# A mixture-of-experts tail on one core: the experts' rows are added by accumulating scatters to x that was stored before, in place of a gather, a weighting pass and a store behind the last expert

## The reference, cut to what matters

```python
h = _layernorm(x) * (1 + cb) + sb              # cb, sb, gb: one row of 128 values per batch
logits = h @ Wg                                 # 8 experts
vals, idx = top_k(softmax(logits), 2)
w = vals / (sum(vals) + 1e-9)                   # two weights per token
# each (token, choice) pair takes the next of 256 places of its expert, or none if it is full
for e in range(8):
    ye = gelu(h @ W1[e] + b1[e]) @ W2[e] + b2[e]    # 128 -> 512 -> 128
    out = out + combine[:, e][:, None] * ye
x = x + gb * out
```

## Time and profile before

| | before |
|---|---|
| median of 3 runs | 833.43 us (833.16 to 837.02) |
| profiled execution, its own time | 835.61 us |
| its span in the trace | 833.9 us |
| busy in the span | PE 718.4, DVE 643.0, POOL 586.7, ACT 491.7 us |
| mean granted TensorE clock | 0.923 |

### The profile page before, as it was taken

One profiled execution on the slowest core, in us unless ns is written; L12 is line 12 of the kernel. 1 busy time (PEld: TensorE's weight loads), 2 busy tenths in 40 slices (PEclk: granted clock), 3 DMA queues, 4 the chain that ended last, 5 costly groups with the idle time before them and its releaser, 6 DMA issues.

```text
span 833.9 us, 34140 instructions
## 1 busy us (share of the span) xinstructions
PE 718.4 (86%) x14802; PEld 655.3 (79%) x14803; DVE 643.0 (77%) x1057; ACT 491.7 (59%) x786; POOL 586.7 (70%) x429
## 2 busy tenths in 40 slices
PE   5577768736799999999999999999999999886997
PEld 2257567725689998988988888889988989785897
DVE  4894645527889999999988999899999999857215
ACT  4766315514675685767577666667766766637520
POOL 4243067866398989898988888888788989831750
PEclk9676659986999999999999999999999999975999
DMA  7832243411052000000000000000000000062128
GB/s 180 234 81 59 55 105 96 88 54 40 5 143 70 7 7 10 7 7 7 6 6 7 23 4 3 4 16 4 4 17 3 4 4 17 17 207 69 49 71 277
DMA packets 61598, 43.01 MB, mean 52 GB/s; under 512 B 22272, under 2 KB 54288, under 8 KB 61456
## 3 DMA queue, kind: packets, MB, share of 16 engines
q1 hardware_dynamic: 58128, 34.07, 14.7%
q0 software_dynamic: 3328, 6.82, 3.4%
HBM read 26.72 MB, written 14.16 MB: 49 GB/s over the span
## 4 chain that ended last, share of the span: by engine, by line
PE 71%; DVE 9%; issue 7%; POOL 5%; ACT 4%; DMA 2%; SPq 1%; POOLq 1%; DVEq 0%; ACTq 0%
PE psum L1875 19%; PE psum L1975 7%; PE psum L1930 7%; PE psum L1908 7%; PE psum L1966 4%; PE psum L1923 4%; PE psum L1937 4%; PE psum L1945 3%; POOL arena L561 2%; PE psum L1673 2%; PE psum L1916 2%; PE psum L2202 2%; PE psum L2226 2%; PE psum L2191 1%; PE psum L1733 1%
## 5 line engine op out<-in xcount | busy, mean ns | idle before, releaser
L1875 PE MATMUL psum<-hT,w_qkv 128*128 128x128 f32 x1408 | 173.4, 280 | 1.7 <-DVE arena L1424 1.2
L1875 PEld LDWEIGHTS psum<-hT,w_qkv 128*128 128x128 f32 x1408 | 164.0, 194 | 4.9 <-DVE arena L1424 1.4
L609 POOL TENSOR_TENSOR arena<-arena,small 128x1024 f32<-128x1024 f32 x56 | 106.0, 1914 | 50.5 <-DVE small L1437 50.5
L588 POOL TENSOR_TENSOR arena<-arena 128x1024 f32<-128x1024 f32 x56 | 106.7, 1906 | 12.4 <-ACT arena L952 12.1
L574 POOL TENSOR_TENSOR arena<-arena 128x1024 f32<-128x1024 f32 x56 | 106.6, 1903 | 0.0
L1430 DVE TENSOR_REDUCE small<-arena 128x16 f32<-128x1024 f32 x60 | 73.1, 1218 | 9.5 <-ACT arena L941 7.3
L613 POOL TENSOR_TENSOR arena<-arena 128x1024 f32<-128x1024 f32 x28 | 65.9, 2353 | 14.6 <-DVE arena L1457 14.5
L1418 DVE TENSOR_REDUCE small<-psum 128x16 f32<-128x1024 f32 x60 | 72.8, 1214 | 3.4 <-PE psum L1975 3.3
L921 ACT ACTIVATE arena<-psum 128x1024 f32<-128x1024 f32 x28 | 28.7, 1026 | 72.6 <-PE psum L1875 72.6
L561 POOL DMA_INDIRECT arena<-h_rows,route x40 | 40.3, 1008 | 43.9 <-DVE route L1275 32.0
L1424 DVE TENSOR_TENSOR arena<-psum,small 128x1024 f32<-128x1024 f32 x60 | 70.4, 1214 | 0.1
(11 more groups left out here) (325 smaller groups left out, 1651.2 us busy)
## 6 DMA issues: line engine op xcount, KB each, us to landing
y_rows<-hT SPq DMA_DIRECT2D x8, 512.0 KB, 6.4
arena<-y_rows SPq DMA_DIRECT2D x8, 512.0 KB, 7.1
o_rows<-arena SPq DMA_DIRECT2D x9, 256.0 KB, 2.4
x_sb<-in_L_attn_u SPq DMA_DIRECT2D x8, 256.0 KB, 4.4
arena<-in_W_inT SPq DMA_DIRECT2D x16, 128.0 KB
arena<-in_W_out SPq DMA_DIRECT2D x64, 32.0 KB
h_rows<-arena SPq DMA_DIRECT2D x4, 512.0 KB, 3.2
h_rows<-hT SPq DMA_DIRECT2D x8, 256.0 KB, 2.3
```

Source lines behind the costliest of these rows:

```text
L588: pool.tensor_tensor(x3, x3, lr[:, tile_of(t) * 32 + k * H:tile_of(t) * 32 + k * H + H].unsqueeze(2).to_broadcast([P, H, D]), ALU.mult).th ...
L609: pool.tensor_tensor(z4, z4, r3.unsqueeze(3).to_broadcast([P, 8, 2, CH]), ALU.mult).then_inc(done, 1)
L1875: mm = pe.matmul(ps[bank][:, p * P:(p + 1) * P], w_qkv[:, j * HD + p * P:j * HD + (p + 1) * P], hT[:, at:at + P], start=True, stop=True)
```

## The change

- **Output.** `out` has 128 rows more at its front, which take what belongs to no token and are cut off on the host as a slice. SP stores x in it during the attention, chunk by chunk beside h (`store_x`), and 128 rows of x into the front; the zero fill of `y_dram`, the read back, the final pass, `x_final` and the last stores are gone. `store_rows` issues two DMAs per chunk in place of one, since rows now lie in token order.
- **Scatter.** `scatter_rows` adds to `out` in DRAM (`compute_op=ALU.add`). As a token has two experts, POOL now waits before each expert's pair for the pair before it to have landed. `AHEAD` is 5.
- **Weights by place.** What is scattered must be weighted and gated. POOL splits the weights into three bf16 parts and multiplies them into the one-hot choice (`weights_by_slot`), ahead of its wait for the ids and of the gathers. PE runs a second pass of 64 products over `pos_hot` (`weights_of_slots`) behind the ids pass and behind POOL; four dummy products follow in place of 18. DVE puts each place's weight under its batch (`batch_of_slot`), PE turns that (`turn_weights`). SP copies the gates to 16 rows per batch with 8 DMAs, ACT makes 16 tables of them (`gate_tables`), and `slots_second` has one more product of 256 columns per expert, which gives weight times gate. DVE has one more multiplication per expert.
- **Layer 0.** The bf16 one-hot is computed directly, before the f32 one; `columns(1)` goes behind the ids pass.

The diff's core:

```diff
-AHEAD = 6
+AHEAD = 5
...
-            sp.wait_ge(x_added, 1)
-            for n in range(2 * BP):
-                r0 = P + n * NC * P
-                sp.dma_start(y_dram[r0:r0 + NC * P, :].rearrange("(t p) c -> p t c", p=P),
-                             hT[:, T * P:(T + 1) * P].unsqueeze(1).to_broadcast([P, NC, C])).then_inc(y_zeroed, 16)
...
             def store_rows(c):
                 sp.wait_ge(h_ready, c + 1)
-                sp.dma_start(h_dram[1].rearrange("(b t p) c -> p b t c", b=BP, p=P)[:, :, c, :], second_rows(c)[0]).then_inc(h_stored[0], 16)
+                for h in range(2):
+                    sp.dma_start(by_chunk(h_dram[1], h, c), second_rows(c)[0][h * CH:(h + 1) * CH]).then_inc(h_stored[0], 16)
+
+            def store_x(c):
+                for h in range(2):
+                    sp.dma_start(by_chunk(A["out"][P:, :], h, c), group_tiles(c)[1][h * CH:(h + 1) * CH]).then_inc(x_stored, 16)
 
             for c in range(NC - 1):
                 store_rows(c)
+                store_x(c)
+            sp.dma_start(A["out"][0:P, :], x_sb[:, 0:C]).then_inc(x_stored, 16)
...
+            store_x(NC - 1)
+            sp.wait_ge(wk_set, BP + 1)
+            for b in range(B):
+                at = b % 2 * CH
+                sp.dma_start(gate_rows[b:P:B, :], mod_of(1, b // 2, GB)[at:at + 2 * E]).then_inc(gates_in, 16)
+            sp.wait_ge(x_stored, 32 * NC + 16)
             for u in range(2):
                 sp.wait_ge(y_scattered[u], 16 * E)
-            for n in range(2 * BP):
-                sp.dma_start(back1[:, n // 2 * 2 * W8:(n // 2 + 1) * 2 * W8].rearrange("p (k h x) -> p k h x", k=2, h=2)[:, :, n % 2, :],
-                             y_dram[P:, :].rearrange("(p k n t) c -> p k n (t c)", k=2, n=2 * BP, t=NC // 2)[:, :, n, :]
-                             ).then_inc(y_half[n][0], 16)
...
-            pool.wait_ge(h_stored[0], 32 + 16 * NC)
+            te = lambda ap: ap.rearrange("p (t e) -> p t e", e=E)
+            over_e = lambda ap: ap.unsqueeze(2).to_broadcast([P, ap.shape[1], E])
+
+            def weights_by_slot():
+                parts = weight_parts.rearrange("p (m t) -> p m t", m=3)
+                chain.link(pool.tensor_copy(parts[:, 0], wk[:, :]))
+                chain.link(pool.tensor_tensor(weight_rest, wk[:, :], parts[:, 0], ALU.subtract))
+                chain.link(pool.tensor_copy(parts[:, 1], weight_rest))
+                chain.link(pool.tensor_tensor(weight_rest, weight_rest, parts[:, 1], ALU.subtract))
+                chain.link(pool.tensor_copy(parts[:, 2], weight_rest))
+                chain.link(pool.tensor_tensor(part_w.rearrange("p (m j t) -> p m j t", m=3, j=2),
+                                             parts.unsqueeze(2).to_broadcast([P, 3, 2, 2 * T]),
+                                             of_tile.rearrange("p (j t) -> p j t", j=2).unsqueeze(1).to_broadcast([P, 3, 2, 2 * T]), ALU.mult))
+                for n in range(6):
+                    last = pool.tensor_tensor(te(weight_rhs[:, n * 2 * T * E:(n + 1) * 2 * T * E]), te(oh1),
+                                             over_e(part_w[:, n * 2 * T:(n + 1) * 2 * T]), ALU.mult)
+                last.then_inc(rhs_ready, 1)
+
+            pool.wait_ge(wk_set, BP + 1)
+            pool.wait_ge(rhs_ready, 5)
+            weights_by_slot()
+            pool.wait_ge(h_stored[0], 32 + 32 * NC)
             pool.wait_ge(ids_set, BP + 1)
             def fetch_rows(e):
 
@@ -697,14 +721,16 @@
             def scatter_rows(e):
 
                 pool.wait_ge(o_ready, TILES0 + 1 + e + 1)
+                if e > 0:
+                    pool.wait_ge(y_scattered[(e - 1) % 2], 32 * ((e - 1) // 2 + 1))
                 apart(pool)
                 for t in range(2):
-                    pool.indirect_dma_start(y_dram[:, :], rows_of(ids_i, e + (2 * E + E * t)), o1_st[e][:, t * C:(t + 1) * C], None,
-                                            bounds_check=P + 2 * B * L - 1, oob_is_err=False).then_inc(y_scattered[e % 2], 16)
+                    pool.indirect_dma_start(A["out"][:, :], rows_of(ids_i, e + (2 * E + E * t)), o1_st[e][:, t * C:(t + 1) * C], None,
+                                            bounds_check=P + B * L - 1, oob_is_err=False, compute_op=ALU.add).then_inc(y_scattered[e % 2], 16)
...
-            def make_weights(n):
-                k, bp = divmod(n, BP)
...
             act.wait_ge(wk_set, BP + 1)
-            for n in range(2 * BP):
-                make_weights(n)
+            act.wait_ge(gates_in, 16 * B)
+            for e in range(E):
+                for j in range(2):
+                    r = j * E + e
+                    last = act.activation(gate_tables[:, (2 * e + j) * C:(2 * e + j + 1) * C], gate_rows, ACT.Copy, scale=table_mask[:, r:r + 1])
+                last.then_inc(tables_made, 1)
...
+            dve.tensor_tensor(te(onehot_b), te(pick), over_e(m2), ALU.is_equal).then_inc(rhs_ready, 1)
             chain.link(dve.tensor_tensor(te(onehot), te(pick), over_e(m2), ALU.is_equal))
-            dve.tensor_copy(onehot_b, onehot).then_inc(rhs_ready, 1)
...
+            def batch_of_slot():
+                by_b = lambda ap: ap.rearrange("p (r b) -> p r b", b=B)
+                chain.link(dve.tensor_tensor(by_b(slot_w), slot_row.unsqueeze(2).to_broadcast([P, 2 * E, B]),
+                                             batch_from.unsqueeze(1).to_broadcast([P, 2 * E, B]), ALU.subtract))
+                chain.link(dve.tensor_scalar(slot_mask, slot_w, 0.0, None, ALU.is_ge))
+                chain.link(dve.scalar_tensor_tensor(slot_w, slot_w, float(L), slot_mask, ALU.is_lt, ALU.mult))
+                dve.wait_ge(ids_mm, 3)
+                chain.link(dve.tensor_reduce(slot_weight, ps[0][:, 512:512 + 6 * E].rearrange("p (m r) -> p r m", m=3), AX_X, ALU.add))
+                dve.tensor_tensor(by_b(slot_w), by_b(slot_w), slot_weight.unsqueeze(2).to_broadcast([P, 2 * E, B]),
+                                  ALU.mult).then_inc(slot_weighed, 1)
...
-                dve.tensor_tensor(o1_st[e].rearrange("p (t c) -> p t c", c=C),
-                                  ps[3][:, u * 512:u * 512 + 2 * C].rearrange("p (t c) -> p t c", c=C),
-                                  over_tiles(b2b[:, e * C:(e + 1) * C], 2), ALU.add).then_inc(o_ready, 1)
+                chain.link(dve.tensor_tensor(o1_st[e].rearrange("p (t c) -> p t c", c=C),
+                                             ps[3][:, u * 512:u * 512 + 2 * C].rearrange("p (t c) -> p t c", c=C),
+                                             over_tiles(b2b[:, e * C:(e + 1) * C], 2), ALU.add))
+                dve.tensor_tensor(o1_st[e], o1_st[e], ps[3][:, u * 512 + 256:u * 512 + 512], ALU.mult).then_inc(o_ready, 1)
...
-            pe.wait_ge(mod_out, 1 + 2 * BP)
-            columns(1)
...
             mm.then_inc(ids_mm, 1)
+            pe.wait_ge(mod_out, 1 + 2 * BP)
+            columns(1)
...
+                pe.wait_ge(slot_weighed, 2)
+                pe.wait_ge(tables_made, e + 1)
+                pe.matmul(ps[3][:, u * 512 + 256:u * 512 + 512], slot_wT, gate_tables[:, e * 2 * C:(e + 1) * 2 * C], start=True, stop=True)
...
-            keep_warm(18, ps[2][:, 0:P])
+            def weights_of_slots():
+                pe.wait_ge(rhs_ready, 6)
+                for t in range(2 * T):
+                    mm = pe.matmul(ps[0][:, 512:512 + 6 * E], hot_of(pos_hot, t),
+                                   weight_rhs.rearrange("p (n t e) -> p n t e", n=6, e=E)[:, :, t, :],
+                                   start=(t == 0), stop=(t == 2 * T - 1))
+                mm.then_inc(ids_mm, 1)
...
+            def turn_weights():
+                pe.wait_ge(slot_weighed, 1)
+                pe.transpose(ps[0][:, 640:640 + P], slot_w, ident[:, :]).then_inc(slot_turned, 1)
+
+            weights_of_slots()
+            keep_warm(4, ps[2][:, 0:P])
             pe.wait_ge(f1_b, 64)
             turn_slots(0)
+            turn_weights()
             slots_first(0)
             turn_slots(1)
...
-            keep_warm(48, ps[0][:, 0:P])
...
```

More of the change, by code:

```diff
@@ L244, in program @@
         slots_in = [sem(f"slots_in{e}") for e in range(AHEAD)]
[L245 to L246 removed]
+        x_stored, slot_weighed, slot_turned, tables_made, gates_in = (
+            sem(n) for n in ("x_stored", "slot_weighed", "slot_turned", "tables_made", "gates_in"))
         y_scattered = [sem(f"y_scattered{u}") for u in range(2)]
@@ L487, in _ @@
             chain.link(pool.iota(edges, pattern=[[P, T]], base=0, channel_multiplier=0, **imprecise))
-            chain.link(pool.iota(pair_no[:, :], pattern=[[T, 2], [1, NC], [NC, BP]], base=P, channel_multiplier=0, **imprecise))
+            for h in range(2):
+                chain.link(pool.iota(pair_no[h * CH:(h + 1) * CH, :], pattern=[[0, 2], [1, NC], [2 * NC, BP]], base=P + (NC - 1) * h,
+                                     channel_multiplier=0, **imprecise))
```

(20 more changed lines are left out.)

67 lines of the change are left out of this document (22 added, 45 removed).

## The result

| | before | after |
|---|---|---|
| median of runs on one chip, us | 833.62 (832.06 to 837.02, 6 runs) | 839.70 (836.46 to 841.01, 6 runs) |
| profiled execution: own time / span, us | 835.61 / 833.9 | 839.88 / 838.1 |
| granted clock, mean | 0.923 | 0.908 |

The ratio is 1.006, 95% interval 1.0036 to 1.0084: slower by 0.6%, where I forecast 828 us and a range of 820 to 838. A second timing, on another chip, gave 1.0045 (1.0015 to 1.0074), so the size lies near half a per cent.

The account below looks back on a forecast made before the run. TensorE was taken to bound 759 to 833.9 us. Removing 24.2 us of read back, final pass and store, against a later first result and longer scatters, gave span 828.6, median 828 us; range 820 to 838.

Parts of the forecast that it names:

- term 6: Scatters to program end: three rounds of 5.29 us, then rounds of 4.2; first to last scatter start 34.0, end at 828.9.
- Rounds above 5.3 from the start: Sign that the forecast is wrong; it expected scatter rounds of 5.3, 5.3, 5.3, then 4.2 us.
- the accumulating scatter is dear: Rival, chance 0.13: in the scatter-land-scatter chain each us of d above 0.5 costs 5, slower by over 0.5% from d = 2.1.
- d: What an accumulating scatter takes beyond a plain one, in the scatter rounds: taken as 0.5 us, bounds zero and 1.5.
- Term 1: POOL's operand beside the tables of places: twelve operations sum to 9.8 us, bounds 7.4 and 15.
- Term 2: Shared memory access of POOL and DVE: table operations and POOL's multiplications don't overlap, 4.9 us more, POOL ends at 774.1.
- Terms 3 to 5: TensorE up to the first result: second pass and dummies shift 8.6 us, clock 1.8, per-expert work 0.5 + 0.4; result at 791.5.
- Term 4: TensorE's clock: part of expert 0 runs at half speed after standing still, 1.8 us, bounds 0 and 4.
- Term 7: Gate copies on ACT, SP's x stores replacing the zero fill, and DVE's mask reduction: all put at nothing.
- Term 8: Layer 0 routing: a cast of 0.29 leaves the path to the first gather; gain 0.3 us.

## Why the prediction was wrong, step by step

- **The failing step is term 6, the scatters,** and in it the sizes. "Rounds above 5.3 from the start" was the prediction's own sign of being wrong, and they are 6.5. The mechanism, a chain of scatter, landing, scatter that did not exist before, was the right one and is the rival that came true, "the accumulating scatter is dear". The term said 34.0; it is 45.5. I had bounded what accumulating costs as a single d at the landing, at most 1.5. It was 1.0 there, inside the bounds. What I had left at the plain scatter's value was the issue on POOL: 1.57 in place of 1.0. That is 1.23 in each of the three early rounds, which I had said would stay at 5.29, 0.57 in each late one and 0.57 between the last two DMAs. The wake behind a landing I put at 0.1; it is 0.75. I had the earlier trace rows with 0.86 from the written ids to the first gather before me and used it in the first part, but not here. Late rounds: 4.2 + 0.57 of issue + 0.5 of landing + 0.65 of wake = 5.9, measured 6.0, times four.
- **The end,** 7.4 in place of 3.2, was not in the sum. I took 0.4 from landing to end; it is 3.6 to the end of POOL's drain, which the final pass had hidden in before, and 0.5 more. It is the cover that I asked about elsewhere and not here.
- **Term 1** (operand 9.8): measured 11.7, 0.9 of it waits that belong to term 2. The five small operations took 0.56 to 0.63 each, where I had 0.3 as an estimate below the 0.46 of 128 columns. All ran beside the tables, so no run shows how much of that is contention. The six of 512 columns took 7.03 against 6.9, and would take 6.3 at the 1.05 of those that met nothing.
- **Term 2** (4.9 of blocking on POOL): the mechanism was right, the size was not. POOL waited 0.9 in its multiplications, and DVE 1.9 in the tables and 0.7 to 0.9 in each of four small operations. I had all eight tables shut POOL out, but six of them ran beside its small operations and took 0.69 to 0.79 in place of 0.68. So the operand was ready 11.9 behind the start of the tables, between the 9.8 of full overlap and the 14.7 forecast. The Trainium skill, "SBUF — State Buffer", section "Who interferes with whom", has the instruction that comes first hold the shared pair. By that rule, the trace agrees: the multiplications that came second took 1.39, 1.50 and 1.18 in place of 1.05, and DVE's operations that came second ended 0.03 to 0.08 (small ones) and 0.55 (tables) behind POOL's.
- **Terms 3 to 5:** the second pass was over 16.1 behind the start of the tables instead of 19.5: 2.8 of that is POOL, 0.7 the pass itself (4.1 against 4.8). The dummies took 2.1 where I had 1.5. The first product ran at full clock here: the granted clock was 0.50 until 774 and 1.00 from 776. Term 4 (1.8) cost nothing in this trace, 0.8 to 0.9 in three others, and turned up as I had described it, 1.8 us, in the kernel where DVE makes the operand. That it was nothing here was luck as far as the runs show. First result 27.2 behind the start of the tables against 32.1. Scatter 0 starts 0.9 behind its result, where I had 0.2.
- **Term 7:** gate tables, stores of x and DVE's mask cost nothing, as said. The zero fill was not free to have: it cost 2 to 3 us at its place, and so its going was a gain that the sum lacked, of a size at the end that stays open.
- **Term 8:** layer 0's routing took 18.50 us against 18.80. Right, 0.30.
- **The range** ended at 838, with the dear scatter left out at a chance of 0.13. Two costs of one mechanism were counted as one, and the point from which it decides (2.1) was thought to be needed at the landing alone. In a late round three separate sizes reached it together: 0.57 of issue, 1.0 of landing and 0.65 of wake, 2.2 beyond the plain scatter with the wake that I had given it. Without the luck ahead of scatter 0 the miss would have been larger.

No version that I ran and that computes the whole output is faster than before. The plain scatter shows what the design would bring without accumulating (0.6%), but it leaves out the sum.

## What to carry to other kernels

When a transfer becomes a link of a chain, price all its parts: the time that it holds its engine, its landing, the wake of the next one, and whatever end-of-stage drain now stands behind it. A sum that only prices "the DMA" misses the engine's share. When an edit takes away the last stage, look at what that stage was hiding. And where the part that two kernels share drifts by several us, compare the stretch that differs from a common mark: two traces of one kernel agreed within 0.3 us from the tables on (81.0 and 81.3, 79.3 twice), though kernels with the same tail gave up to 82.0, while whole executions of one kernel were 7 and 8 us apart. Look at single rows, too, before calling an engine undisturbed: a mean of 1.17 hid operations of 1.05 and 1.50.

## What the runs showed of the hardware

- An accumulating indirect DMA of 64 KB holds GpSimd for 1.57 us and lands after 3.3; a plain one 0.98 and 2.3.
- A GpSimd drain behind indirect DMAs ends 5.3 us behind the last one's issue, accumulating or plain, and takes 5.27 when it starts two us later; behind arithmetic, in layer 0, one took 3.34.
- From a landing to the start of the next indirect DMA that waits for it, 0.75 us.
- Beside GpSimd's multiplications, VectorE's operations of 16 columns took 0.94 to 1.10 us in place of 0.17 to 0.23, and two of its eight table operations 1.41 and 1.54 in place of 0.68. GpSimd's multiplications of 512 columns took 1.39 and 1.50 beside the tables and 1.05 behind them; the same lengths stand in all seven traces in which GpSimd makes the operand.
- TensorE fell to half clock again in the midst of the experts, after it had stood from 804 to 806 for a late gather. Granted clocks of after, in stretches of 2 us:

```profile
804.00:806.00 2.00, 0.00 (x0) 0.00 (x0) 0.00 (x0) 1.57 (x4) 1.70 (x2) 1.00 0.19 53
806.00:808.00 2.00, 1.83 (x7) 1.66 (x8) 0.42 (x1) 0.00 (x0) 1.69 (x2) 0.50 0.39 40
808.00:810.00 2.00, 2.00 (x14) 2.00 (x14) 0.00 (x0) 0.00 (x0) 0.36 (x1) 0.65 0.36 33
```
